# Part 3 of a four-layer kernel: the routed expert picked from exponentials, one gate of the cross attention moved to ScalarE, 12 instead of 13 keys in ScalarE's share, and a new order of steps

## The reference, cut to what matters

```python
# x3: additive cross attention over 77 keys, 64 sequences
txt_proj  = ctx @ Ws                                  # 77 x 128 for each sequence
feat_proj = features @ W                              # 128 x 128, features = layernorm(x)
h   = tanh(txt_proj[:, None, :] + feat_proj[None, :, :] + b)   # every token with every key
rho = h @ w + (1 - q_mask) * -1e30
att = softmax(rho)
w_s = tanh((att @ ctx) @ Wcw + bcw)                   # one gate for each token
b_s = tanh((att @ ctx) @ Wcb + bcb)                   # a second one
x   = x + (w_s * features + b_s)
# f3: mixture of 8 experts, top 1, with a capacity
probs = softmax(xt @ wg);  idx = argmax(probs)        # xt = layernorm(x)
mask  = one_hot(idx) * (place of the token in its expert < capacity)
gate  = sum(probs * mask)
x     = x + gate * (xt @ W[idx].T + b[idx])           # nothing for tokens over capacity
```

## Time and profile before

| | us |
|---|---|
| median of 3 runs | 3202.42 (3200.71 to 3205.06) |
| the profiled execution, its own time | 3210.65 |
| its span | 3208.9 |
| part 3 within the span | about 2281 to 3209 |
| DVE busy over the span | 2658.8 (83%) |
| PE busy | 2783.6 (87%) |
| ACT busy | 2508.3 (78%) |
| POOL busy | 828.6 (26%) |

### The profile page before, as it was taken

One profiled execution on the slowest core, in us unless ns is written; L12 is line 12 of the kernel. 1 busy time (PEld: TensorE's weight loads), 2 busy tenths in 40 slices (PEclk: granted clock), 3 DMA queues, 4 the chain that ended last, 5 costly groups with the idle time before them and its releaser, 6 DMA issues. The chain is left out here.

```text
span 3208.9 us, 78310 instructions
## 1 busy us (share of the span) xinstructions
PE 2783.6 (87%) x28057; PEld 2002.6 (62%) x28057; DVE 2658.8 (83%) x7379; ACT 2508.3 (78%) x6617; POOL 828.6 (26%) x1437
## 2 busy tenths in 40 slices
PE   6999899999999759979999997876688888888887
PEld 4666666666666536656767674334566667667665
DVE  4899898999989525459999995788599999999995
ACT  4999899999999525547777773687599998999995
POOL 1233233333333100025555541000122221222221
PEclk7999999999999669989999997998789998999997
DMA  1011311111111011101111111001200000000000
GB/s 47 26 33 33 78 33 33 33 30 31 32 33 33 14 54 42 43 22 33 35 34 35 34 33 30 1 0 32 69 10 15 15 15 15 14 15 15 15 15 8
DMA packets 176000, 91.15 MB, mean 28 GB/s; under 512 B 46243, under 2 KB 171877, under 8 KB 175619
## 3 DMA queue, kind: packets, MB, share of 16 engines
q1 hardware_dynamic: 170084, 76.85, 8.9%
q0 software_dynamic: 4096, 8.40, 0.8%
q10 hardware_dynamic: 1440, 0.90, 0.1%
HBM read 43.73 MB, written 42.36 MB: 27 GB/s over the span
## 5 line engine op out<-in xcount | busy, mean ns | idle before, releaser
L2299 DVE TENSOR_TENSOR th<-tf 128x2048 f32<-128x2048 f32 x256 | 583.5, 2279 | 12.1 <-PE p_rho L2203 8.1
L2149 ACT ACTIVATE th<-th 128x2048 f32<-128x2048 f32 x256 | 488.9, 1911 | 6.8 <-DVE th L2299 6.8
L643 ACT ACTIVATE probf<-probf,colf 128x128 f32<-128x128 f32 x1024 | 314.4, 403 | 0.0
L2203 PE MATMUL p_rho<-th,late_w_row 128*32 128x128 f32 x8192 | 301.6, 285 | 13.1 <-ACT th L2149 13.1
L613 ACT ACTIVATE prob<-prob,col 128x77 f32<-128x77 f32 x1024 | 270.0, 352 | 4.6 <-DVE col L896 4.6
L2160 ACT ACTIVATE tl<-tf 128x128 f32<-128x128 f32 x832 | 256.9, 390 | 0.0
L2203 PEld LDWEIGHTS p_rho<-th,late_w_row 128*32 128x32 f32 x8192 | 229.4, 113 | 28.3 <-ACT th L2149 17.8
L1755 PE MATMUL acc<-xnT_all,wT 128*128 128x512 f32 x384 | 181.3, 625 | 29.6 <-DVE tmax L1947 13.2
L791 PE MATMUL fp<-ident,probf 128*128 128x128 f32 x1024 | 145.0, 287 | 27.3 <-ACT ygf L650 24.6
L942 DVE TENSOR_TENSOR probf<-fs,causal 128x1024 f32<-128x1024 f32 x128 | 153.7, 1201 | 16.9 <-PE fs L779 16.9
L2264 PE MATMUL p_f<-w_pair,xm 128*128 128x128 f32 x1024 | 166.8, 330 | 0.0
(11 more groups left out here) (432 smaller groups left out, 7964.2 us busy)
## 6 DMA issues: line engine op xcount, KB each, us to landing
rows<-zeros SPq DMA_DIRECT2D x64, 256.0 KB, 2.4
cxT<-in_ctxT SPq DMA_DIRECT2D x128, 38.5 KB, 2.0
xb<-rows SPq DMA_DIRECT2D x67, 64.0 KB, 1.8
rows<-yb SPq DMA_DIRECT2D x67, 64.0 KB, 1.5
x<-in_x SPq DMA_DIRECT2D x64, 64.0 KB, 1.8
x_mid<-x SPq DMA_DIRECT2D x64, 64.0 KB, 1.5
z<-x_mid SPq DMA_DIRECT2D x64, 64.0 KB
x_next<-z SPq DMA_DIRECT2D x64, 64.0 KB, 1.5
```

Of the source, the lines that this page charges most:

```text
L643: last = nc.scalar.activation(scores, scores, ACT.Exp, bias=colf[s][:, 16 + HALF * hf + h:17 + HALF * hf + h])
L2149: nc.scalar.activation(b[:], b[:], ACT.Tanh).then_inc(act_done, ACT_L.did(f"t{c}.tanh", e))
L2203: last = nc.tensor.matmul(p_rho[r][ROWS * b:ROWS * (b + 1), 0:TOK], w_row[:, ROWS - 1 - a:2 * ROWS - 1 - a], tanh[:, k, :], start=(a == 0) ...
L2299: nc.vector.tensor_tensor(th[i % NT][:], tf[s][:, n * KT:(n + 1) * KT].unsqueeze(2).to_broadcast([128, KT, TOK]), tf[s][:, FEAT:FEAT + TOK ...
```

## The change

- **The pick.** `f3.emax` goes; `f3.eq` compares each exponential with 1.0 (is_ge) instead of with the largest. `f3.gate` goes too: `f3.out` multiplies with the reciprocal of the sum (column 18) alone.
- **The gates.** `x3.y` and `x3.x` become one instruction, `x3.x`: `x = xn * w_s + x`. The second gate is added by a new step of ScalarE, `x3.shift`, an Identity activation over the 128x128 tile with column 23 as its bias; it waits for `x3.gate` and for `f3.norm` of the same sequence, and `f3.out` waits for it. (A number that is the same for all features of a token does not change the token's layer norm.)
- **The keys.** The fourth chunk has 17 keys (2176 columns), ScalarE's own share 12 (6 and 6).
- **The order.** All four texts are new. Lines of part 3 move by up to 6.

```diff
+PE_D = """
+    r.rho1@2 f3.route@5 r.rho2@2 p.gate@3 r.rho3@2 r.rhoT@2 f3.place@5 f3.kT@5 r.rho0@1 f3.g@5 x3.T x3.proj f3.y@5
+    r.rhoL@1 p.PT@2 f3.T@4
+"""
 ACT_D = """
...
+    f3.exp@5 ta.tanh@1 x3.rho@2 t0.tanh@1 f3.kT@5 t1.tanh@1 x3.xT x3.exp@2 tb.tanh@1 x3.proj x3.shift@5 t2.tanh@1
+    x3.gate@3 f3.xT@4 t3.tanh@1 x3.PT@2
 """
...
 POOL_D = """
-    f3.rstd@4 x3.eps x3.rstd f3.eps@3
+    f3.rstd@5 x3.eps x3.rstd f3.eps@4
 """
...
+                act.wait_ge(act_done, ACT_L.value("x3.gate", e))
+                act.wait_ge(dve_done, DVE_L.value("f3.norm", e))
+                nc.scalar.activation(x[e % NR][:], x[e % NR][:], ACT.Identity, bias=col[s][:, 23:24]).then_inc(act_done, ACT_L.did("x3.shift", e))
+                yield
...
-                nc.vector.tensor_scalar(xn[s][:], xn[s][:], c[:, 22:23], c[:, 23:24], ALU.mult, ALU.add).then_inc(dve_done, DVE_L.did("x3.y", e))
-                yield
-                after("x3.y", e)
-                nc.vector.tensor_tensor(x[q][:], x[q][:], xn[s][:], ALU.add).then_inc(dve_done, DVE_L.did("x3.x", e))
+                nc.vector.scalar_tensor_tensor(x[q][:], xn[s][:], c[:, 22:23], x[q][:], ALU.mult, ALU.add).then_inc(dve_done, DVE_L.did("x3.x", e))
...
-                nc.vector.tensor_reduce(c[:, 19:20], c[:, 24:32], X_AXIS, ALU.max).then_inc(dve_done, DVE_L.did("f3.emax", e))
-                yield
...
-                after("f3.emax", e)
-                nc.vector.scalar_tensor_tensor(c[:, 32:40], c[:, 24:32], c[:, 19:20], first[:], ALU.is_equal, ALU.mult).then_inc(dve_done, DVE_L.did("f3.eq", e))
+                nc.vector.scalar_tensor_tensor(c[:, 32:40], c[:, 24:32], 1.0, first[:], ALU.is_ge, ALU.mult).then_inc(dve_done, DVE_L.did("f3.eq", e))
...
-                after("f3.rden", e)
-                nc.vector.tensor_tensor(c[:, 21:22], c[:, 18:19], c[:, 19:20], ALU.mult).then_inc(dve_done, DVE_L.did("f3.gate", e))
...
+                dve.wait_ge(act_done, ACT_L.value("x3.shift", e))
+                nc.vector.scalar_tensor_tensor(x[q][:], p_f[:, 256:256 + DIM], c[:, 18:19], x[q][:], ALU.mult, ALU.add).then_inc(dve_done, DVE_L.did("f3.out", e))
```

More of the change, by code:

```diff
@@ L186 @@
 """
+PE_D = """
+    r.rho1@2 f3.route@5 r.rho2@2 p.gate@3 r.rho3@2 r.rhoT@2 f3.place@5 f3.kT@5 r.rho0@1 f3.g@5 x3.T x3.proj f3.y@5
+    r.rhoL@1 p.PT@2 f3.T@4
+"""
 ACT_D = """
-    f3.kT@5 tb.tanh@1 x3.PT@3 t1.tanh@1 x3.rho@2 t0.tanh@1 x3.gate@3 x3.xT f3.xT@4 ta.tanh@1 f3.exp@4 x3.proj
-    t2.tanh@1 x3.exp@2 t3.tanh@1
+    f3.exp@5 ta.tanh@1 x3.rho@2 t0.tanh@1 f3.kT@5 t1.tanh@1 x3.xT x3.exp@2 tb.tanh@1 x3.proj x3.shift@5 t2.tanh@1
+    x3.gate@3 f3.xT@4 t3.tanh@1 x3.PT@2
 """
 DVE_D = """
[L192 to L198, removed]
+    x3.rden@3 x3.sum0@1 f3.nmax@5 x3.sum1@1 f3.rden@5 f3.eq@5 x3.x@4 f3.first@5 x3.gb@3 f3.pick@5 f3.taken@5
+    f3.stats@4 x3.stats f3.aggr@4 f3.keep@5 x3.aggr x3.sum2@1 x3.norm x3.nmax@2 f3.xm@5 f3.norm@4 x3.sum3@1 f3.out@5
 """
 POOL_D = """
-    f3.rstd@4 x3.eps x3.rstd f3.eps@3
+    f3.rstd@5 x3.eps x3.rstd f3.eps@4
 """
@@ L2024, in part_3 @@
     ROWS = 32
-    CHUNKS = 4
-    TAIL = KEYS - CHUNKS * KT
-    KPAD = (CHUNKS + 1) * KT
+    CHUNK = (0, KT, 2 * KT, 3 * KT, 4 * KT + 1)
+    CHUNKS = len(CHUNK) - 1
+    TAIL = KEYS - CHUNK[-1]
+    KPAD = 80
     WIDE = 4 * ROWS
@@ L2049, in part_3 @@
         cg = ring(NX, "cg3", [KEYS, 2])
-        th = ring(NT, "th3", [128, KT, TOK])
+        th = ring(NT, "th3", [128, KT + 1, TOK])
         tl = ring(2, "tl3", [128, TAIL, TOK])
@@ L2147, in chain @@
                     act.wait_ge(dve_done, DVE_L.value(f"x3.sum{c}", e))
-                    b = th[(CHUNKS * e + c) % NT]
-                    nc.scalar.activation(b[:], b[:], ACT.Tanh).then_inc(act_done, ACT_L.did(f"t{c}.tanh", e))
+                    b = th[(CHUNKS * e + c) % NT][:, 0:CHUNK[c + 1] - CHUNK[c], :]
+                    nc.scalar.activation(b, b, ACT.Tanh).then_inc(act_done, ACT_L.did(f"t{c}.tanh", e))
                     yield
@@ L2159, in chain @@
                     for k in keys:
-                        last = nc.scalar.activation(tl[r][:, k, :], tf[s][:, FEAT:FEAT + TOK], ACT.Tanh, bias=tf[s][:, CHUNKS * KT + k:CHUNKS * KT + k + 1])
+                        last = nc.scalar.activation(tl[r][:, k, :], tf[s][:, FEAT:FEAT + TOK], ACT.Tanh, bias=tf[s][:, CHUNK[-1] + k:CHUNK[-1] + k + 1])
                     last.then_inc(act_done, ACT_L.did(f"{p}.tanh", e))
@@ L2176, in f3 @@
                 yield
-            go_through(ACT_L, dict(x3=x3, t0=chunk(0), t1=chunk(1), t2=chunk(2), t3=chunk(3), ta=tail("ta", range(0, 7)), tb=tail("tb", range(7, TAIL)), f3=f3))
+            go_through(ACT_L, dict(x3=x3, t0=chunk(0), t1=chunk(1), t2=chunk(2), t3=chunk(3), ta=tail("ta", range(0, TAIL // 2)), tb=tail("tb", range(TAIL // 2, TAIL)), f3=f3))
         @block.tensor
@@ L2203, in add @@
                         last = nc.tensor.matmul(p_rho[r][ROWS * b:ROWS * (b + 1), 0:TOK], w_row[:, ROWS - 1 - a:2 * ROWS - 1 - a], tanh[:, k, :],
-                                                start=(a == 0), stop=(a == CHUNKS * KT // 4 - 1), tile_position=(0, ROWS * b))
+                                                start=(a == 0), stop=(CHUNK[-1] - 4 <= first_key + k < CHUNK[-1]), tile_position=(0, ROWS * b))
                     return last
@@ L2210, in rho @@
                         pe.wait_ge(act_done, ACT_L.value("x3.rho", e - 2))
-                    add(c * KT, th[(CHUNKS * e + c) % NT], KT).then_inc(pe_done, PE_L.did(f"r.rho{c}", e))
+                    add(CHUNK[c], th[(CHUNKS * e + c) % NT], CHUNK[c + 1] - CHUNK[c]).then_inc(pe_done, PE_L.did(f"r.rho{c}", e))
                     yield
@@ L2215, in rho @@
                         pe.wait_ge(act_done, ACT_L.value("tb.tanh", e))
-                        add(CHUNKS * KT, tl[r], TAIL).then_inc(pe_done, PE_L.did("r.rhoL", e))
+                        add(CHUNK[-1], tl[r], TAIL).then_inc(pe_done, PE_L.did("r.rhoL", e))
                         yield
@@ L2291, in x3 @@
                 if e >= NX:
-                    after("x3.y", e - NX)
+                    after("x3.x", e - NX)
                 yield from norm("x3", e, c, xn[s])
@@ L2298, in x3 @@
                         dve.wait_ge(pe_done, PE_L.value(f"r.rho{(i - NT) % CHUNKS}", (i - NT) // CHUNKS))
-                    nc.vector.tensor_tensor(th[i % NT][:], tf[s][:, n * KT:(n + 1) * KT].unsqueeze(2).to_broadcast([128, KT, TOK]),
-                                            tf[s][:, FEAT:FEAT + TOK].unsqueeze(1).to_broadcast([128, KT, TOK]), ALU.add).then_inc(dve_done, DVE_L.did(f"x3.sum{n}", e))
+                    shape = [128, CHUNK[n + 1] - CHUNK[n], TOK]
+                    nc.vector.tensor_tensor(th[i % NT][:, 0:shape[1], :], tf[s][:, CHUNK[n]:CHUNK[n + 1]].unsqueeze(2).to_broadcast(shape),
+                                            tf[s][:, FEAT:FEAT + TOK].unsqueeze(1).to_broadcast(shape), ALU.add).then_inc(dve_done, DVE_L.did(f"x3.sum{n}", e))
                     yield
@@ L2361, in f3 @@
                 yield
-                after("f3.gate", e)
+                after("f3.rden", e)
                 dve.wait_ge(pe_done, PE_L.value("f3.y", e))
-                nc.vector.scalar_tensor_tensor(x[q][:], p_f[:, 256:256 + DIM], c[:, 21:22], x[q][:], ALU.mult, ALU.add).then_inc(dve_done, DVE_L.did("f3.out", e))
+                dve.wait_ge(act_done, ACT_L.value("x3.shift", e))
+                nc.vector.scalar_tensor_tensor(x[q][:], p_f[:, 256:256 + DIM], c[:, 18:19], x[q][:], ALU.mult, ALU.add).then_inc(dve_done, DVE_L.did("f3.out", e))
                 yield
```

## The result

The changed kernel takes 3396.5 us (median of 4, 3392.3 to 3404.3) against 3201.6 of the kernel before, measured together: a ratio of 1.0615 (95% interval 1.0598 to 1.0631). It is slower, as forecast, and by 195 us instead of 48. The profiled execution spans 3398.1 us, the one before 3208.9.

The account below looks back on a forecast made before the run. VectorE's own work was taken to bound part 3 at 13.22 us a turn; the change's ring of 13.95 gives 0.73 x 59 = +43, ends +2, clock +3: 3202.4 + 48 = 3250 us, range 3221 to 3273.

Parts of the forecast that it names:

- The new wait on VectorE: In part 3, x3.norm waits for GpSimd behind the chunk x3.sum2: 3.03 us from chunk to norm instead of 2.20, +0.83 a turn.
- VectorE's and ScalarE's own work: Work per turn of part 3 without waits: VectorE 13.22 to 12.76 us, ScalarE 12.87 to 12.97 us.
- hold: VectorE's chunk x3.sum2 holds back GpSimd's x3.eps until it ends: 2.17 us instead of 0.22, in every turn.
- The ring: Loop through ScalarE, PE and VectorE from x3.xT round to x3.xT sets part 3's turn: 13.95 us, 13.12 without the hold.
- The clock: TensorE's half-clock stretches delay f3.out through f3.y: between -15 and +16 us in all, taken as +3.
- the 31.6: Waits of f3.out for f3.y in part 3 of the earlier trace, 31.6 us in 17 waits, put down to half clock.
- 1: Hold there, but VectorE alone sets part 3's turn at 13.59 us (or x3.rstd is caught instead): 3226 us, chance 0.15.
- 2 (no hold): GpSimd's x3.eps gets through before the chunk in steady turns: 3198 us, or 3189 with cheaper x3.shift; chance 0.13.
- 3: The 0.46 us a turn removed from VectorE is a gain only if nothing else is as late; no separate chance given.
- the ends: Part 3's first turns, draining turns and later last f3.out: +2 us together in the main forecast.

Follow-up runs that it names:

- e6: Changed kernel plus unread matmuls on PE ahead of five waits (8, 5, 6, 16 ahead of x3.T, 5): 3231.4 us, ratio 1.0088.
- e12: Changed kernel with x3.stats and x3.aggr earlier on VectorE, plus unread PE matmuls ahead of four waits, none ahead of x3.T: 3181.3 us, ratio 0.9948.
- e2: Kernel before with f3.xm moved ahead of x3.aggr on VectorE, nothing else: 3236.1 us, ratio 1.0103.
- e4: Kernel before with the change's four edits but its old order, x3.nmax and f3.aggr ahead of f3.rden: 3194.9 us, ratio 0.9983.
- e11: e4 plus unread matmuls on PE, 12 ahead of r.rho2, 13 ahead of f3.g, 3 ahead of x3.T: 3157.0 us, ratio 0.9866.
- e3: Changed kernel plus 16 unread matmuls on PE ahead of x3.T's wait for x3.norm: 3346.0 us, ratio 1.0458.
- e7: Changed kernel with f3.y cut to 8 of its 16 matmuls, experts 4 to 7 left out of the result: 3326.7 us, ratio 1.0378.
- e10: Kernel before plus unread matmuls on PE ahead of r.rho2 (4), f3.g (7), p.gate (4), f3.y (5), x3.T (3): 3172.8 us, ratio 0.9915.
- e1: Changed kernel with x3.stats and x3.aggr moved up on VectorE, well ahead of the chunk x3.sum2: 3314.7 us, ratio 1.0359.
- e8: Changed kernel with e1's order and all of e6's unread matmuls, including the 16 ahead of x3.T: 3221.3 us, ratio 1.0061.

## Why the prediction was wrong, step by step

- **The new wait on VectorE: right.** 2.17 and 0.77 us as read off the start of the part, +0.83 forecast, 0.84 (full-clock turns of e6 and e12) and 0.86 (e2) measured.
- **VectorE's and ScalarE's own work: right.** With hold and clock out of the way the edits in the old order run at ScalarE's forecast 12.97 us (e4, e11), and `x3.shift` takes 0.41 us of duration and 0.31 of spacing, where I took 0.30.
- **The ring: right in kind, 0.2 short.** 13.95 forecast, 14.17 in e6; without the hold 13.12 forecast, 13.33 in e12. The 0.2 is one term, from `x3.rho` to `f3.keep`, put at 1.0: it is 1.20 in e6 (2710.96 to 2712.16) and in the changed kernel, which has no fillers (2711.00 to 2712.20). The others came as forecast, `x3.xT` to `x3.rho` at 8.99 for 9.0.
- **The clock: this step failed.** I wrote that it would come to "between -15 (half of the 31.6 gone) and +16 (half as much again), I take +3". In the old order slow stretches cost 13.71 - 13.22 = 0.49 us a turn (mean less full-clock turn); in the new one 17.07 - 14.17 = 2.90. The difference, 2.4 us over some 57 turns, is 137 us where the sum has 3: 134 of the 147 missing. The rest is the ring's 0.2 (12 us).

Three things in that step were wrong. "The longer turn asks less of PE" was put down as a relief. It is the opposite: a PE with less to do is the one whose clock falls, as e3, e6 and e7 show from both sides (more work, full clock; less work, 0.74). And "almost no reserve" was priced at half as much again on the old number of slow stretches, when both factors changed, how often the clock falls and what a fall costs. The profile of before already had the rows for the second:

```profile
2705.34 3.78 PE L2264 MATMUL p_f<-w_pair,xm 128*128 128x128 f32 x16
...
2720.61 2.05 PE L2264 MATMUL p_f<-w_pair,xm 128*128 128x128 f32 x16
```

That is 1.7 us more at half clock for `f3.y`; `x3.proj`, `r.rhoL` and `f3.T`, newly next to it on PE, show 0.6, 0.5 and 0.2 more in the same two turns. That sum for one slow turn is 3 us, 59 of them 177, less the 28 that the old order pays already: an estimate of about +150 that belonged in the range as its upper bound. For how often it falls the row would have been one of PE, turn by turn: in the new text `r.rhoT`, `f3.place`, `f3.kT`, `r.rho0`, `f3.g` and `x3.T` follow each other, short steps and one chunk, four of them behind waits (0.56, 0.35, 0.45 and 1.07 us in the changed trace), and the heavy ones come in a block after them. The old text has them mixed. I took single durations only from the earlier trace rows. And the earlier trace rows was misread as what the clock costs: of its 31.6 us, 16.5 in 5 waits lie in the last five turns, where the pipeline drains and where e10 has 13.7 too. The clock's cost in 58 turns, 0.49 each, is 28 us; that this is near 31.6 is luck.

**How the parts add up.** From the times: new order and edits at full clock without hold 3181 (e12); letting the clock fall +133 (e1, 3315); the hold on top +82 (3396). The mean turns over 58 turns are free of what parts 1 and 2 took: 13.45, 15.85 and 17.04, so +139 and +69 us (those parts ended 14 us earlier in e1 than in the changed kernel). Of the 69, 43 are the hold's cost at full clock (e6 against e12) and 26 the step from slow turns in part of the cases to slow turns in all. The two together cost more than each alone.

The rivals: 1 (VectorE alone sets the turn at 13.59) was not seen. 2 (no hold) was not seen either. 3 has its point: at full clock and without the hold the new order with the edits is 8 us behind the old order without them (3181.3 against 3172.8). A slip in rival 1's sum changed nothing: 22, 2 for the ends and 3 for the clock give 3229, not 3226.

What stays open is what about the new order makes the clock fall, apart from how much PE has to do: whether the light stretch's place ahead of the heavy one or its length alone decides wasn't tried.

## What to carry to other kernels

Before moving steps about, lay out TensorE's turn as well, even if it is not the full engine: where its light steps gather in one place, its clock can fall right behind them, and then whatever comes next takes nearly twice as long; price that for every turn, not for as many as the old trace shows. A few matmuls nobody reads, in front of waits, are a cheap test for it: if the granted clock rises and the time falls with it, the clock was the cause. If the time does not fall, the test says little, since fillers without a wait to stand in cost time themselves (0.56 us a turn for 16 in e8). And where an addition with two SBUF inputs stands between a GpSimd instruction and the one that waits for it, GpSimd is behind the whole addition.

## What the hardware showed that was not expected

- The clock falls on a PE that is never idle for long. In the changed kernel its longest wait in the turn is 1.07 us, and in the 4.4 us before the fall it is busy 2.52. In the kernel before, PE is busy 3.46 of the 4.6 us ahead of a fall (2700.0 to 2704.6), with no wait longer than 0.47. The Trainium skill tells of such an oscillation (TensorE: Matmul & The Clock Gate, "HAM oscillation — how this bites in real kernels"), where each tile's wait puts the next tile at half clock. The repetition is the same here; the waits are far shorter than the ones it tells of.
- Fillers in the waits hold the clock at 1.00 over the steady part, and make a kernel faster by more than many a change of its work: 27 us for the kernel before (3200.1 to 3172.8), 165 for the changed one.
- A pipeline can fall into step with the clock: 58 falls, each 17.07 us after the last, and a turn that came 0.5 us late made it up. A shorter chain then need not shorten the turn: with `f3.T` earlier it stayed at 17.07 us, and with half of `f3.y` the clock's share fell from 0.80 to 0.74.
- `x3.eps` on GpSimd takes 2.17 us behind a chunk in every turn, as at the start. In e1, where `f3.eps` runs into the chunk instead, it takes 2.24 us, and VectorE waits for it once, 0.3 us.
